# A graph layer's edge rounds on VectorE in another row order, with slot indices decoded in two rounds and 112 first gathers

## The chip, the cores and the metric

The kernel runs on one core of a Trainium2 chip. Five engines matter: TensorE (PE in the profile; PEld is its weight load), VectorE (DVE), ScalarE (ACT), GpSimd (POOL) and SyncE (SP, which only issues transfers). Each works through its own list of instructions in order and waits on semaphores for the others. The metric is device time of one execution in microseconds (us); smaller is better.

## What is computed

A pre-normalised graph layer over 100,000 nodes of 160 features (64 scalars and 32 three-vectors) and 25,000 edges, all in fp32:

```python
h = relu(layernorm(x))                                  # per node, 160 features
s, v = h[:, :64], h[:, 64:].reshape(N, 32, 3)
skip_s, skip_v = s @ W_skip0, einsum('nmi,mk->nki', v, W_skip1)
s, v = s @ W_nl0, einsum('nmi,mk->nki', v, W_nl1)
sh1  = sqrt(3) * edge_attr / norm(edge_attr)            # unit vector of an edge
w    = relu(edge_feature @ W_fc1) @ W_fc2               # 224 weights of an edge, split in 5
xs, xv = s[dst], v[dst]
tp   = concat(w0*xs, w3*dot(xv, sh1)/sqrt(3), (w1*xs) x sh1, w2*xv, w4*cross(xv, sh1)/sqrt(2))
agg  = segment_sum(tp, src) / 32                        # sum over the edges of a node
out_s, out_v = agg_s @ W_out_s + skip_s, agg_v @ W_out_v + skip_v
out  = x + concat(silu(out_s[:, :64]), sigmoid(out_s[:, 64:]) * out_v)
```

## The kernel before

The program has three stages on one time axis.

**Ranking, until about 123 us.** The 25,000 edges stand as 200 tiles of 125 (`NT = 200`). PE and DVE count, tile by tile, how many earlier edges fall into the same bin of nodes; from this rank each edge gets a row of its own in the DRAM tensor `slots`. Meanwhile POOL gathers the node rows of the first edges from `x` by indirect DMA, one call per tile (`gather`, L502), into rings called `xg` and `xb`.

**Edge rounds, about 124 to 590 us.** Four tiles make a group (`GE = 4`, `NG = 50` groups), and all engines run a loop of 53 rounds q, each engine on another group. On DVE `stats_e` takes the layer-norm statistics of a gathered group. For two groups at a time `spread_e`, `squares_e`, `variance_e` (in even rounds) and `guess_e`, `newton_a` to `newton_c`, `shift_e` (in odd rounds) make scale and bias; these are operations on 8 elements per partition, and the last of them, `shift_e`, writes `e_bias` (L685). ACT normalises with it (`norm_e`, L1178, waiting for the semaphore `e_ln`), PE turns and multiplies, and leaves the transformed rows in a PSUM bank (L1329, L1333; semaphore `e_xs`). `products` on DVE then forms the 352 numbers of an edge from the rows in PSUM (`row_s`, `row_v`), the edge's weights `w_sb` and its unit vector `hat` in SBUF: four operations (L853 to L860) read one operand from PSUM and one from SBUF, the eight after them (L864 to L880) read both operands from SBUF. PE projects the result, ACT puts it into a message buffer, and `lift` and `complete` on DVE add one more part to a message of an earlier group (L888, L895, both operands in SBUF) and copy its indices in (L896), which raises `e_fix`.

Then POOL may scatter: `scatter(p)` (L512) waits for `e_fix` of group p and makes four indirect DMA calls, one per tile, from the message buffer into `slots`. POOL's list of calls is written out by hand. First come `FIRST_GATHERS` gather calls. Then POOL waits for the slot indices `sidx` (semaphore `b_slot`, raised by the last of four `slot_rows` steps on DVE, one step at the end of each of the rounds 0 to 3), and goes on with four scatters for each p, followed by the gathers up to `due`:

```python
for p in range(NG):
    scatter(p)
    due = min(NT, max(FIRST_GATHERS + 2 * (p + 1), GE * (p + 10)))
    for m in range(made, due):
        gather(m)
```

With 104 first gathers this is two gathers after each p up to 33 and four after each p from 34 to 40, when all 200 are made; after that only scatters follow. So POOL makes 96 gathers and 200 scatters after the wait for `sidx`.

**Node tiles, from about 590 us.** SP waits until all scatters have landed, loads the slots of each macro tile of 1024 nodes (`mg`), and PE, ACT and DVE compute skip, sum, gate and residual for 98 such tiles. Their instructions are not touched by the change.

Of the kernel before, what the change touches and what calls it, by code (L numbers as in the profile page):

```python
# [5 lines left out]
ALU = mybir.AluOpType  # L6
# [12 lines left out]
def gnn_layer(nc, x, src, dst, edge_vec, edge_feat_t, w_skip0, w_skip1, w_nl0, w_nl1,  # L19
# [10 lines left out]
    GE = 4  # L30
# [36 lines left out]
    FIRST_GATHERS = 104  # L67
# [3 lines left out]
    with ExitStack() as ctx:  # L71
# [289 lines left out]
        with ExitStack() as psum_ctx:  # L361
# [124 lines left out]
            def _(pool):  # L486
# [44 lines left out]
                for p in range(NG):  # L531
                    scatter(p)
                    due = min(NT, max(FIRST_GATHERS + 2 * (p + 1), GE * (p + 10)))
                    for m in range(made, due):
                        gather(m)
                    made = max(made, due)
# [49 lines left out]
            def _(dve):  # L586
# [109 lines left out]
                for t in range(NT):  # L696
# [58 lines left out]
                    if t == 90:  # L755
                        stats_e(2)
                    if t == 100:
# [85 lines left out]
                def products(p, c):  # L843
                    rows = f_x if p == 0 else p_x
                    row_s, row_v = rows[:, :, 0:S], rows[:, :, S:F].rearrange("p t (i k) -> p t i k", i=3)
                    w = w_sb[:, c, :, :]
                    h = hat[:, p * GE:p * GE + GE, :]
                    h3 = h[:, :, 0:3].unsqueeze(3)
                    dve.wait_ge(e_wsb, p + 1)
                    dve.wait_ge(e_xs, p + 1)  # L850
                    wait(dve, e_tp, p)
                    wait(dve, e_tt, GE * (p - 1))
                    dve.tensor_tensor(w4xv[:], w[:, :, W - V:W].unsqueeze(2).to_broadcast((ET, GE, 3, V)),  # L853
                                      row_v, ALU.mult).then_inc(e_w4xv, 1)
                    dve.tensor_tensor(xvh[:], h3.to_broadcast((ET, GE, 3, V)), row_v, ALU.mult).then_inc(e_dot, 1)
                    parts = tp[:, c, :, V + 2 * S:TU].rearrange("p t (i k) -> p t i k", i=3)
                    dve.tensor_tensor(tp[:, c, :, V:V + 2 * S].rearrange("p t (j k) -> p t j k", j=2),
                                      w[:, :, 0:2 * S].rearrange("p t (j k) -> p t j k", j=2),
                                      row_s.unsqueeze(2).to_broadcast((ET, GE, 2, S)), ALU.mult)
                    dve.tensor_tensor(parts[:, :, :, 0:V],  # L860
                                      w[:, :, 2 * S:2 * S + V].unsqueeze(2).to_broadcast((ET, GE, 3, V)),
# [701 lines left out]
```

## Time and profile before

| | |
|---|---|
| median of 3 runs | 1210.98 us (1209.78 to 1215.87) |
| profiled execution | 1209.0 us |
| its span in the profile | 1207.2 us |
| busy share of the span | PE 92%, PEld 78%, DVE 81%, ACT 71%, POOL 60% |
| last scatter call of POOL ends | 586.9 us |
| first load of `mg` issued | 590.5 us |

Times in the rows are counted from the start of the span. A row of the timeline gives the start of an instruction, its duration, the engine, the line, what it does (out <- in, partitions x elements), and in brackets how long the engine stood idle before it and what ended that. POOL shows 0.30 us "issue" ahead of nearly each indirect DMA call: it waits there for nothing that the profile shows. A DVE operation's duration overlaps the start of the next by about 0.08 us in a run of operations that wait for nothing.

### The profile page before, as it was taken

Reading aid. Unit: us, or ns where it says so; the run is one execution under the profiler, and the core shown is the slowest. Engines: PE = TensorE matmul, PEld = TensorE weight load, DVE = VectorE, ACT = ScalarE, POOL = GpSimd, SP = SyncE. Lnnn points to the kernel's source line nnn. Section 1 sums busy time; section 2 is a strip of 40 time slices with the busy share of each in tenths; the row PEclk is TensorE's granted clock in tenths of the full one; section 3 lists DMA queues with packets and bytes.
Section 4 is the critical chain, followed back from the end, with each engine's and each line's share of the span. In section 5 each row is a group of like instructions: output and inputs, shape, how many; then the busy total and the mean of one; then the engine's idle time right before and its main releaser. Section 6 shows DMA issues by size and latency. Waiting matters only on the chain.

```text
span 1207.2 us, 29282 instructions
## 1 busy us (share of the span) xinstructions
PE 1115.1 (92%) x8847; PEld 939.8 (78%) x8847; DVE 979.8 (81%) x3571; ACT 860.4 (71%) x2069; POOL 729.7 (60%) x860
## 2 busy tenths in 40 slices
PE   6989899999999767889699999999999999999996
PEld 4667788888888656778588788888888788888885
DVE  9999898888886447667488888888888888888874
ACT  0300578877777445566598899899888898889984
POOL 6777587787887777777615544554445544554460
PEclk9999899999999788789599999999999999999999
DMA  9999344444446633444387777777777677777763
GB/s 343 404 403 403 119 131 132 129 131 130 130 129 195 214 104 101 114 113 123 106 296 275 259 286 281 282 255 284 284 282 285 247 286 279 285 265 282 286 214 118
DMA packets 108459, 271.12 MB, mean 225 GB/s; under 512 B 13573, under 2 KB 51751, under 8 KB 108364
## 3 DMA queue, kind: packets, MB, share of 16 engines
q1 hardware_dynamic: 87852, 233.20, 54.9%
q0 software_dynamic: 19200, 36.48, 10.4%
q8 instruction: 45, 0.74, 0.2%
q10 hardware_dynamic: 1312, 0.29, 0.1%
q14 instruction: 50, 0.41, 0.1%
HBM read 126.91 MB, written 143.01 MB: 224 GB/s over the span
## 4 chain that ended last, share of the span: by engine, by line
PE 62%; DVE 12%; POOL 12%; issue 8%; DMA 3%; ACT 2%; SPq 0%; DVEq 0%; POOLq 0%; ACTq 0%
PE bank L1465 16%; PE bank L1478 9%; PE bank L1457 8%; POOL slots L512 7%; PE bank L1469 5%; POOL xg L502 5%; PE bank L1394 4%; PE bank L1297 3%; PE bank L1423 3%; PE bank L1329 3%; DVE ob L1047 2%; PE bank L1411 2%; DVE bin_hot L626 2%; PE bank L1407 2%; PE bank L1409 2%
## 5 line engine op out<-in xcount | busy, mean ns | idle before, releaser
L1246 ACT ACTIVATE nn<-xb,n_bias,n_rstd 128x160 f32<-128x160 f32 x784 | 346.2, 528 | 45.3 <-POOL n_bias L567 40.9
L512 POOL DMA_INDIRECT slots<-msg,sidx x200 | 229.3, 1147 | 75.5 <-issue 56.1
L956 DVE BATCH_NORM_STATS2 n_stat<-xb 128x6 f32<-128x160 f32 x784 | 196.0, 312 | 24.8 <-DMA xb<-x 24.2
L1047 DVE SCALAR_TENSOR_TENSOR ob<-sg,bank 128x128 f32<-128x128 f32 x588 | 131.7, 279 | 72.4 <-ACT ob L1261 70.7
L1478 PE MATMUL bank<-mg,hot 64*128 64x192 f32 x1568 | 171.8, 338 | 7.7 <-DVE hot L1032 7.7
L544 POOL TENSOR_TENSOR n_sum<-n_stat 128x32 f32<-128x32 f32 x24 | 6.9, 287 | 279.5 <-DVE n_stat L956 279.5
L502 POOL DMA_INDIRECT xg<-x,dst_i x136 | 145.7, 1072 | 44.0 <-issue 41.0
L561 POOL TENSOR_TENSOR n_rstd<-n_sum,neg_half 128x8 f32<-128x8 f32 x94 | 160.2, 1704 | 5.7 <-issue 2.9
L1465 PE MATMUL bank<-fwd,nt 128*128 128x160 f32 x784 | 144.6, 307 | 14.3 <-DVE ob L1047 12.4
L1253 ACT ACTIVATE nt<-bank 128x640 f32<-128x640 f32 x196 | 137.5, 702 | 18.1 <-PE bank L1458 14.1
L1054 DVE TENSOR_TENSOR ob<-ob,xb 128x1280 f32<-128x1280 f32 x98 | 146.9, 1499 | 3.4
L1457 PE MATMUL bank<-ident,nn 128*128 128x128 f32 x784 | 146.9, 310 | 2.6 <-ACT nn L1246 2.6
L1457 PEld LDWEIGHTS bank<-ident,nn 128*128 128x128 f32 x784 | 109.1, 207 | 46.9 <-issue 46.1
L1465 PE MATMUL bank<-rev,nt 128*128 128x160 f32 x784 | 139.1, 300 | 0.0
L1394 PE MATMUL bank<-ident,tp 125*128 125x125 f32 x600 | 108.3, 291 | 29.4 <-ACT tpt L1202 18.5
L1465 PEld LDWEIGHTS bank<-fwd,nt 128*128 128x128 f32 x784 | 113.0, 191 | 26.1 <-issue 13.4
L1478 PEld LDWEIGHTS bank<-mg,hot 64*128 64x128 f32 x1568 | 124.4, 188 | 7.9 <-DVE hot L1032 7.9
L1394 PEld LDWEIGHTS bank<-ident,tp 125*128 125x128 f32 x600 | 70.9, 150 | 64.3 <-issue 25.8
L1202 ACT ACTIVATE tpt<-bank 128x375 f32<-128x375 f32 x200 | 96.3, 482 | 31.9 <-PE bank L1394 31.5
L1465 PEld LDWEIGHTS bank<-rev,nt 128*128 128x128 f32 x784 | 117.7, 191 | 0.0
L638 DVE BATCH_NORM_STATS2 e_stat<-xg 125x6 f32<-125x160 f32 x136 | 37.1, 313 | 66.8 <-DMA xg<-x,dst_i 66.8
L1178 ACT ACTIVATE hn<-xg,e_bias,e_rstd 125x160 f32<-125x160 f32 x136 | 63.4, 523 | 37.0 <-DVE e_bias L685 37.0
(191 smaller groups left out, 2669.9 us busy)
## 6 DMA issues: line engine op xcount, KB each, us to landing
xb<-x SPq DMA_DIRECT2D x97, 640.0 KB, 5.1
out_dram<-ob SPq DMA_DIRECT2D x97, 640.0 KB, 3.3
slots<-blank SPq DMA_DIRECT2D x14, 2744.0 KB
mg<-slots SPq DMA_DIRECT2D x98, 392.0 KB, 4.0
messages<-msg SPq DMA_DIRECT2D x50, 382.8 KB
ef<-edge_feat_t SPq DMA_DIRECT2D x50, 125.0 KB
slots<-msg,sidx POOLq DMA_INDIRECT x200, 4.1
xg<-x,dst_i POOLq DMA_INDIRECT x136, 6.8
```

Of the source, the lines that this page charges most:

```text
L502: pool.indirect_dma_start(rows_of(g)[:, t, :], None, x[:, :], bass.IndirectOffsetOnAxis(ap=dst_i[:, m:m + 1], axis=0)).then_inc(e_x[g % XS ...
L512: pool.indirect_dma_start(slots[:, :], bass.IndirectOffsetOnAxis(ap=sidx[:, m:m + 1], axis=0), msg[:, c, t, 0:MW], None).then_inc(e_sc[c], 16)
L561: pool.tensor_tensor(n_rstd[:, b, cols], n_sum[:, b, 4, cols], neg_half[:], ALU.pow).then_inc(n.chain, 1)
L956: done = dve.bn_stats(n_stat[:, u // U, u % U * G + g, :], xb[:, u, g, :])
L1047: last = dve.scalar_tensor_tensor(out=o[:, :, S + V * j:S + V * j + V], in0=sg[:, h, :, :], scalar=1.0, in1=z[:, :, part], op0=ALU.add, op ...
L1054: dve.tensor_tensor(o, o, xb[:, u, :, :], ALU.add).then_inc(n.res, 1)
L1246: last = act.activation(nn[:, u % 2, h, spread_of(g % 4)], xb[:, u, g, order_of(g % 4)], ACT.Relu, bias=n_bias[:, u // U, c:c + 1], scale= ...
L1253: act.activation(nt[:, h, :], q_t[h], ACT.Relu).then_inc(n.ht, 1)
L1394: last = pe.transpose(p_tt[:, i * ET:(i + 1) * ET], tp[:, c, t, TURN[i]:TURN[i] + P], idt)
L1457: pe.transpose(q_t[h][:, t * P:(t + 1) * P], nn[:, u % 2, h, main_of(t)], ident[:])
L1465: pe.matmul(z[:, t, 0:F], nt[:, h, t * P:(t + 1) * P], sides[t // 2][:, skip_cols], start=(t % 2 == 0), stop=False, skip_group_check=True)
L1478: last = pe.matmul(q_z[h][:, t, 0:Z], hot[slots, u % 2, pair, :], mg[slots, u % U, pair, 0:Z], start=False, stop=True, skip_group_check=True)
```

## The change

Nothing is computed differently; instructions stand in another order. Four things move.

1. `FIRST_GATHERS` is 112 in place of 104, and `due` has `p + 11` in place of `p + 10`.
2. Two of the four `slot_rows` steps stand at the end of round 0 and two at the end of round 1, so `sidx` is written at the end of round 1 and not of round 3.
3. `stats_e(3)` moves from round 0 into the ranking stage (at t = 96; `stats_e(2)` from t = 90 to t = 88), and each round takes the statistics of group q + 4 as its last work where the next round took them as its first.
4. `products`, `lift` and `complete` are dissolved into one round body. Their operations and the small ones alternate, so that the four that read PSUM stand between those whose operands are both in SBUF.

The core of the diff, cut:

```diff
-    FIRST_GATHERS = 104
+    FIRST_GATHERS = 112
...
-                    due = min(NT, max(FIRST_GATHERS + 2 * (p + 1), GE * (p + 10)))
+                    due = min(NT, max(FIRST_GATHERS + 2 * (p + 1), GE * (p + 11)))
...
-                    if t == 90:
+                    if t == 88:
                         stats_e(2)
+                    if t == 96:
+                        stats_e(3)
...
                 def round_e(q):
-                    m = q // 2 + 1
...
-                    if within(q - 1):
-                        products(q - 1, (q + 1) % 2)
-                    if q < 4:
-                        slot_rows(q)
+                    p, c, m = q - 1, (q + 1) % 2, q // 2 + 1
+                    root, spread = q % 2 == 1 and within(q + 1), q % 2 == 0 and within(q + 3)
+                    r = q - 3
+
+                    if root:
+                        guess_e(m)
+                    if spread:
+                        spread_e(m)
+                    if within(r):
+                        h3 = hat[:, r * GE:r * GE + GE, 0:3].unsqueeze(3).to_broadcast((ET, GE, 3, V))
+                        v = msg[0:ET, r % MR, :, SG:Z].rearrange("p t (i k) -> p t i k", i=3)
+                        dve.wait_ge(e_msb, 2 * r + 2)
+                        wait(dve, e_fix, r)
+                        dve.tensor_tensor(hu[:], msg[0:ET, r % MR, :, Z:Z + V].unsqueeze(2).to_broadcast((ET, GE, 3, V)), h3,
+                                          ALU.mult).then_inc(e_hu, 1)
+                    if root:
+                        newton_a(m)
+                    if spread:
+                        squares_e(m)
+                    if within(p):
+                        rows = f_x if p == 0 else p_x
+                        row_s, row_v = rows[:, :, 0:S], rows[:, :, S:F].rearrange("p t (i k) -> p t i k", i=3)
+                        w = w_sb[:, c, :, :]
+                        h = hat[:, p * GE:p * GE + GE, :]
+                        parts = tp[:, c, :, V + 2 * S:TU].rearrange("p t (i k) -> p t i k", i=3)
+                        dve.wait_ge(e_wsb, p + 1)
+                        dve.wait_ge(e_xs, p + 1)
+                        wait(dve, e_tp, p)
+                        wait(dve, e_tt, GE * (p - 1))
+                        dve.tensor_tensor(xvh[:], h[:, :, 0:3].unsqueeze(3).to_broadcast((ET, GE, 3, V)), row_v, ALU.mult
+                                          ).then_inc(e_dot, 1)
+                    if root:
+                        newton_b(m)
+                    if spread:
+                        variance_e(m)
+                    if within(r):
+                        dve.wait_ge(e_hu, r + 1)
+                        dve.tensor_tensor(v, v, hu[:], ALU.add)
+                        dve.tensor_copy(msg[0:ET, r % MR, :, LOCAL:NODE + 1], place_of[:, r * GE:r * GE + GE, :]).then_inc(e_fix, 1)
+                    if root:
+                        newton_c(m)
+                    if within(p):
+                        dve.tensor_tensor(w4xv[:], w[:, :, W - V:W].unsqueeze(2).to_broadcast((ET, GE, 3, V)),
+                                          row_v, ALU.mult).then_inc(e_w4xv, 1)
+                        dve.wait_ge(e_dot, 3 * p + 1)
+                        dve.tensor_tensor(dot[:, 0, :, :], xvh[:, :, 0, :], xvh[:, :, 1, :], ALU.add).then_inc(e_dot, 1)
+                        dve.tensor_tensor(tp[:, c, :, V:V + 2 * S].rearrange("p t (j k) -> p t j k", j=2),
+                                          w[:, :, 0:2 * S].rearrange("p t (j k) -> p t j k", j=2),
+                                          row_s.unsqueeze(2).to_broadcast((ET, GE, 2, S)), ALU.mult)
+                        dve.wait_ge(e_w4xv, p + 1)
+                        dve.tensor_tensor(cr_a[:, :, 0:2, :], w4xv[:, :, 1:3, :],
+                                          h[:, :, 2:4].unsqueeze(3).to_broadcast((ET, GE, 2, V)), ALU.mult)
+                        dve.tensor_tensor(cr_a[:, :, 2, :], w4xv[:, :, 0, :],
+                                          h[:, :, 1:2].to_broadcast((ET, GE, V)), ALU.mult)
+                    if root:
+                        shift_e(m)
+                    if within(p):
+                        dve.tensor_tensor(parts[:, :, :, 0:V],
+                                          w[:, :, 2 * S:2 * S + V].unsqueeze(2).to_broadcast((ET, GE, 3, V)),
+                                          row_v[:, :, ::-1, :], ALU.mult).then_inc(e_px, 1)
+                        dve.wait_ge(e_dot, 3 * p + 2)
+                        dve.tensor_tensor(dot[:, 1, :, :], dot[:, 0, :, :], xvh[:, :, 2, :], ALU.add).then_inc(e_dot, 1)
+                        dve.tensor_tensor(cr_b[:, :, 0, :], w4xv[:, :, 2, :], h[:, :, 1:2].to_broadcast((ET, GE, V)), ALU.mult)
+                        dve.tensor_tensor(cr_b[:, :, 1:3, :], w4xv[:, :, 0:2, :],
+                                          h[:, :, 2:4].unsqueeze(3).to_broadcast((ET, GE, 2, V)), ALU.mult).then_inc(e_cross, 1)
+                        dve.wait_ge(e_dot, 3 * p + 3)
+                        dve.tensor_tensor(tp[:, c, :, 0:V], dot[:, 1, :, :],
+                                          w[:, :, 2 * S + V:2 * S + 2 * V], ALU.mult)
+                        dve.wait_ge(e_cross, p + 1)
+                        dve.tensor_tensor(parts[:, :, :, V:2 * V],
+                                          cr_a[:, :, ::-1, :], cr_b[:, :, ::-1, :], ALU.subtract).then_inc(e_tp, 1)
+                    if within(q + 4):
+                        stats_e(q + 4)
+                    if q < 2:
+                        slot_rows(2 * q)
+                        slot_rows(2 * q + 1)
```

On DVE, an odd round stood before in this order from `newton_c` (L681) on (`BN_STATS` is the last of its statistics, L685 is `shift_e`, L888 is `lift`, L895 and L896 are `complete`, L853 begins `products`):

```order
L681 SCALAR_TENSOR_TENSOR e_rstd<-e_step,e_rstd 125x8
L638 BN_STATS e_stat<-xg 125x6
L685 SCALAR_TENSOR_TENSOR e_bias<-e_sum,e_rstd 125x8
L888 TENSOR_TENSOR hu<-msg,hat 125x384
L895 TENSOR_TENSOR msg<-msg,hu 125x4x96
L896 COPY msg<-place_of 125x4x2
L853 TENSOR_TENSOR w4xv<-w_sb,bank 125x384
```

and in the changed kernel, from the operation that follows `newton_a` on (L876 was L855, L884 was L895, L885 was L896, L889 was L853, L892 was L864, L893 was L857, L897 and L899 were L867 and L869, L904 was L860):

```order
L876 TENSOR_TENSOR xvh<-hat,bank 125x384
L675 SCALAR_TENSOR_TENSOR e_step<-e_root,e_sum 125x8
L884 TENSOR_TENSOR msg<-msg,hu 125x4x96
L885 COPY msg<-place_of 125x4x2
L681 SCALAR_TENSOR_TENSOR e_rstd<-e_step,e_rstd 125x8
L889 TENSOR_TENSOR w4xv<-w_sb,bank 125x384
L892 TENSOR_TENSOR dot<-xvh 125x128
L893 TENSOR_TENSOR tp<-w_sb,bank 125x4x128
L897 TENSOR_TENSOR cr_a<-w4xv,hat 125x4x64
L899 TENSOR_TENSOR cr_a<-w4xv,hat 125x4x32
L685 SCALAR_TENSOR_TENSOR e_bias<-e_sum,e_rstd 125x8
L904 TENSOR_TENSOR tp<-w_sb,bank 125x4x3x32
```

The bias of the next two groups (L685) stood ahead of all products of its round; now it stands behind `lift`, `complete` and six of the twelve operations of `products`.

The last part of `products` on DVE stood before as eight operations with both operands in SBUF behind the last one that reads PSUM (`bank`):

```order
L860 TENSOR_TENSOR tp<-w_sb,bank 125x4x3x32
L864 TENSOR_TENSOR dot<-xvh 125x128
L867 TENSOR_TENSOR cr_a<-w4xv,hat 125x4x64
L869 TENSOR_TENSOR cr_a<-w4xv,hat 125x4x32
L872 TENSOR_TENSOR dot<-dot,xvh 125x128
L873 TENSOR_TENSOR cr_b<-w4xv,hat 125x4x32
L874 TENSOR_TENSOR cr_b<-w4xv,hat 125x4x64
L877 TENSOR_TENSOR tp<-dot,w_sb 125x4x32
L880 TENSOR_TENSOR tp<-cr_a,cr_b 125x4x3x32
```

and in the changed kernel as

```order
L904 TENSOR_TENSOR tp<-w_sb,bank 125x4x3x32
L908 TENSOR_TENSOR dot<-dot,xvh 125x128
L909 TENSOR_TENSOR cr_b<-w4xv,hat 125x4x32
L910 TENSOR_TENSOR cr_b<-w4xv,hat 125x4x64
L913 TENSOR_TENSOR tp<-dot,w_sb 125x4x32
L916 TENSOR_TENSOR tp<-cr_a,cr_b 125x4x3x32
L638 BN_STATS e_stat<-xg 125x6 x4
```

Three of the eight (L864, L867, L869) moved ahead of the last PSUM operation; five still stand in one run, and the statistics follow them.

On POOL the calls from the end of the ranking stage on stood before as

```order
L524 IOTA sidx 128x200
L502 DMA xg<-x,dst_i 128x160 x66
L502 DMA xb<-x,dst_i 128x160 x36
L512 DMA slots<-msg,sidx 50776x196 x4
L502 DMA xb<-x,dst_i 128x160 x2
```

and now as

```order
L524 IOTA sidx 128x200
L502 DMA xg<-x,dst_i 128x160 x66
L502 DMA xb<-x,dst_i 128x160 x44
L512 DMA slots<-msg,sidx 50776x196 x4
L502 DMA xb<-x,dst_i 128x160 x2
```

(two gathers more stand ahead of the IOTA in both). Eight gathers moved ahead of the first scatter; the end of POOL's list of calls, as a difference, shows where they are gone:

```order
-L512 DMA slots<-msg,sidx 50776x196 x4
-L502 DMA xg<-x,dst_i 128x160 x4
-L512 DMA slots<-msg,sidx 50776x196 x36
+L512 DMA slots<-msg,sidx 50776x196 x40
 L544 TENSOR_TENSOR n_sum<-n_stat 128x32
```

The last gather now follows scatter p = 39 and not p = 40, so 88 gathers and 160 scatters stand between the wait for `sidx` and the last gather, where 96 and 164 stood; 40 scatters follow it, not 36.

## Rows read from the trace of the kernel before

**Rows 1.** Who waited for whom, POOL, 5 to 600 us: total, times, longest.
```profile
POOL slots L512 <- DVE sidx L809: 10.0, 1, 10.0
POOL slots L512 <- DVE msg L896: 9.4, 15, 5.2
```

**Rows 2.** Who waited for whom, all engines, 386 to 532 us: the longest.
```profile
DVE e_stat L638 <- DMA xg<-x,dst_i: 63.2, 11, 9.5
```

**Rows 3.** Timeline of POOL: four of the calls that mark its stages.
```profile
147.82 1.01 POOL L512 DMA_INDIRECT slots<-msg,sidx  x1 [9.97 <-DVE sidx L809]
...
386.05 0.96 POOL L502 DMA_INDIRECT xg<-x,dst_i  x1 [0.31 <-issue]
...
530.75 0.95 POOL L502 DMA_INDIRECT xg<-x,dst_i  x1 [0.30 <-issue]
...
585.97 0.97 POOL L512 DMA_INDIRECT slots<-msg,sidx  x1 [0.30 <-issue]
```

**Rows 4.** Timeline of POOL in two steady rounds: three prolonged calls, one undisturbed.
```profile
202.84 1.32 POOL L512 DMA_INDIRECT slots<-msg,sidx  x1 [0.30 <-issue]
204.47 0.99 POOL L512 DMA_INDIRECT slots<-msg,sidx  x1 [0.30 <-DVE msg L896]
...
207.03 1.90 POOL L512 DMA_INDIRECT slots<-msg,sidx  x1 [0.30 <-issue]
...
222.39 1.93 POOL L512 DMA_INDIRECT slots<-msg,sidx  x1 [0.30 <-issue]
```

**Rows 5.** Timeline of DVE in the same stretch: one odd round.
```profile
202.72 0.56 DVE L888 TENSOR_TENSOR hu<-msg,hat 125x384 f32<-125x384 f32 x1 [0.82 <-ACT msg L1211]
203.32 0.56 DVE L895 TENSOR_TENSOR msg<-msg,hu 125x384 f32<-125x384 f32 x1
203.79 0.34 DVE L896 COPY msg<-place_of 125x8 f32<-125x8 f32 x1
203.87 0.55 DVE L853 TENSOR_TENSOR w4xv<-w_sb,bank 125x384 f32<-125x384 f32 x1
204.33 0.55 DVE L855 TENSOR_TENSOR xvh<-hat,bank 125x384 f32<-125x384 f32 x1
204.79 0.68 DVE L857 TENSOR_TENSOR tp<-w_sb,bank 125x512 f32<-125x512 f32 x1
205.39 0.54 DVE L860 TENSOR_TENSOR tp<-w_sb,bank 125x384 f32<-125x384 f32 x1
205.86 0.28 DVE L864 TENSOR_TENSOR dot<-xvh 125x128 f32<-125x128 f32 x1
206.06 0.41 DVE L867 TENSOR_TENSOR cr_a<-w4xv,hat 125x256 f32<-125x256 f32 x1
206.40 0.28 DVE L869 TENSOR_TENSOR cr_a<-w4xv,hat 125x128 f32<-125x128 f32 x1
206.60 0.28 DVE L872 TENSOR_TENSOR dot<-dot,xvh 125x128 f32<-125x128 f32 x1
...
207.54 0.55 DVE L880 TENSOR_TENSOR tp<-cr_a,cr_b 125x384 f32<-125x384 f32 x1
```

**Rows 6.** Timeline of ACT in the same odd round.
```profile
204.85 0.94 ACT L1178 ACTIVATE hn<-xg,e_bias,e_rstd 125x160 f32<-125x160 f32 x2
206.13 0.48 ACT L1202 ACTIVATE tpt<-bank 128x375 f32<-128x375 f32 x1 [0.33 <-PE bank L1394]
206.73 0.54 ACT L1211 ACTIVATE msg<-bank 125x448 f32<-125x448 f32 x1
207.17 0.93 ACT L1178 ACTIVATE hn<-xg,e_bias,e_rstd 125x160 f32<-125x160 f32 x2
```

**Rows 7.** Timeline of PE: the rows' last product, and the next turn of normalised rows.
```profile
203.23 0.27 PE L1333 MATMUL bank<-rev,ht 64*125 64x64 f32 x1
...
208.18 0.73 PE L1379 MATMUL bank<-ident,hn 125*128 125x125 f32 x4
```

**Rows 8.** Timeline of DVE: the operation that completes the last message.
```profile
578.97 0.30 DVE L896 COPY msg<-place_of 125x8 f32<-125x8 f32 x1
```

More of the change, by code:

```diff
@@ L883, in lift @@
-                def lift(p):
-                    c = p % MR
-                    h3 = hat[:, p * GE:p * GE + GE, 0:3].unsqueeze(3).to_broadcast((ET, GE, 3, V))
-                    dve.wait_ge(e_msb, 2 * p + 2)
-                    wait(dve, e_fix, p)
-                    dve.tensor_tensor(hu[:], msg[0:ET, c, :, Z:Z + V].unsqueeze(2).to_broadcast((ET, GE, 3, V)), h3,
-                                      ALU.mult).then_inc(e_hu, 1)
-                def complete(p):
-                    c = p % MR
-                    v = msg[0:ET, c, :, SG:Z].rearrange("p t (i k) -> p t i k", i=3)
-                    dve.wait_ge(e_hu, p + 1)
-                    dve.tensor_tensor(v, v, hu[:], ALU.add)
-                    dve.tensor_copy(msg[0:ET, c, :, LOCAL:NODE + 1], place_of[:, p * GE:p * GE + GE, :]).then_inc(e_fix, 1)
@@ L898, in round_e @@
-                def round_e(q):
-                    m = q // 2 + 1
-                    if q % 2 == 0:
-                        if within(q + 3):
-                            stats_e(q + 3)
-                            spread_e(m)
-                        if within(q - 3):
-                            lift(q - 3)
-                        if within(q + 3):
-                            squares_e(m)
-                        if within(q - 3):
-                            complete(q - 3)
-                        if within(q + 3):
-                            variance_e(m)
-                    else:
-                        more = within(q + 1)
-                        if more:
-                            guess_e(m)
-                        if within(q + 3):
-                            stats_e(q + 3, range(0, 1))
-                        if more:
-                            newton_a(m)
-                        if within(q + 3):
-                            stats_e(q + 3, range(1, 2))
-                        if more:
-                            newton_b(m)
-                        if within(q + 3):
-                            stats_e(q + 3, range(2, 3))
-                        if more:
-                            newton_c(m)
-                        if within(q + 3):
-                            stats_e(q + 3, range(3, 4))
-                        if more:
-                            shift_e(m)
-                        if within(q - 3):
-                            lift(q - 3)
-                            complete(q - 3)
-                    if within(q - 1):
-                        products(q - 1, (q + 1) % 2)
-                    if q < 4:
-                        slot_rows(q)
```

38 lines of the change are left out of this document (removed).

## The prediction

> **What bounds the kernel now.** I read the waits first, engine by engine, then the chain that ended last, then the timelines of POOL and of the three engines it meets. The node stage after 590 us is untouched by the change and needs the last scatter, so its length stays and the question is when the last scatter ends: at 585.97 + 0.97 = 586.94 us [rows 3]. POOL has nothing to wait for between its first gather and that moment except 10.0 us for `sidx` and 9.4 us for completed messages, of which 5.2 us lie in one wait near the end [rows 1]. From 386 us on it is DVE that waits for gathered rows, 63.2 us in 11 times [rows 2]. So the edge stage is POOL's list of calls; PE, ACT and DVE run ahead of it until the gathers are short, and follow it from then on.
>
> The list has three stretches [rows 3]. The first scatter starts at 147.82, and the call at 386.05 is the 156th after the wait (26 times four scatters and two gathers): 155 calls in 238.2 us, 1.537 us each, while DVE is full. The call after the one at 530.75 starts 0.95 + 0.30 later, at 532.00: 105 calls in 145.95 us, 1.390 each, while DVE is half idle. The last 36 scatters take 54.94 us, 5.2 of it the one wait: 1.383 each. A call that meets nothing costs its 0.95 to 1.01 us and 0.30 us of issue, about 1.28 us.
>
> Why 1.537 and not 1.28: in a steady pair of rounds two kinds of call are prolonged [rows 4]. The one at 202.84 starts 0.12 us into L888 (202.72), and ends at 204.16, 0.88 after L888 [rows 5]. The one at 207.03 starts in the middle of the run from L869 to L880 and ends at 208.93, 0.84 after L880 ended at 208.09. With some 0.98 us for a call by itself they were let in at 203.18 and 207.95, 0.10 and 0.14 us before those operations ended. So a call that starts inside a DVE operation with both operands in SBUF first waits, and in the run from L869 to L880 (208.09 - 206.40 = 1.69 us) it waits for the whole of what is left of the run. The call at 204.47 starts beside L855, which reads PSUM, and takes 0.99. From 207.03 to 222.39, two rounds later, POOL makes 10 calls: 15.36 / 10 = 1.536, the rate of the whole stretch.
>
> At this place the Trainium skill has a rule, in "SBUF — State Buffer", section "SBUF: two separate sides": a VectorE operation with two SBUF inputs and a GpSimd operation that reads SBUF share a port pair as an exclusive lock, held for one whole instruction. The trace agrees that such operations block a call [rows 4, 5]; it disagrees on one instruction, since the call at 207.03 waited through several. By the rule no call would be held longer than one operation, at most 0.55 us, in either order, and the new order would end where the first rival below does; by the rows it can gain in rate only if no run is longer than the 1.28 us between two calls.
>
> **The change part by part.**
>
> *112 first gathers.* POOL was free from 147.82 - 9.97 = 137.85 on. Eight more gathers fill that wait: 8 x 1.25 (0.95 + 0.30) = 10.0 us, so 147.9; DVE is in its first rounds then, and one hit on the run costs up to 1.6 us. I take 149.5 for the first scatter, 1.7 us later than before (bounds 0 and 3). `sidx` is ready earlier and hides behind these gathers: the first message was complete before the last of four steps released POOL at 147.82, and the two steps in round 1 come some 15 us, two rounds, earlier. If it were late after all, it costs at most the two rounds it gained.
>
> *Fewer calls ahead of the last gather.* 88 gathers and 160 scatters, 248 calls, in place of 260; then 40 scatters in place of 36.
>
> *The new DVE order and POOL's rate.* The operations are the same, so the time that locks are held is about the same, but it stands in pieces: `lift` alone, L895 alone (0.47 us each), L864 alone (0.2), L867 and L869 (0.54), and the run from L872 to L880, 208.09 - 206.60 = 1.49 us, of which about 1.37 bar a new call (the last 0.1 did not, above). This run is still longer than 1.28, so each round catches a call in it. After release the next starts follow at 1.28, 2.56, 3.84, 5.12 and 6.40 us; the next run starts one round less 1.37 us later. For a round of 7.68 that is 6.31: the fifth start falls just inside, so five calls per round, as now. What the short pieces add falls into slack ahead of that hit.
>
> *The late bias.* In odd rounds `e_bias` now stands behind xvh, L895, L896, w4xv, L864, L857, L867 and L869. From start to start these take 0.46 + 0.47 + 0.08 + 0.46 + 0.20 + 0.60 + 0.34 + 0.20 = 2.81 us [rows 5], two small operations 0.08 each (as L896 to L853), and I put 0.2 for `shift_e` itself until ACT sees it. xvh can start when the rows are done, 203.23 + 0.27 = 203.50 [rows 7], say 203.65. So the bias is ready at 206.8, where ACT started to normalise at 204.85: 1.95 late. Between ACT's first and second pair of normalisations there are 2.32 us, 0.33 of it idle and about 0.2 more a wait inside 206.13 to 206.73 [rows 6], so the second slips by some 1.4 us. PE's turn at 208.18 came right behind it (207.17 + 0.93 = 208.10), and PE is full: a pair of rounds grows from 15.36 to 16.76 us. Bounds: nothing, if PE's order takes it up, and 1.95. In front of ACT's normalisation then stand its copies for PE (L1202), so PE's projection waits too; that is the same 1.4, not a second one. For POOL a round of 9.08 and one of 7.68 take 6 and 5 calls by the reckoning above (9.08 - 1.37 = 7.71, sixth start at 7.68, at the edge of the run): 11 calls in 16.76, 1.524 each. The change to the order thus leaves POOL's rate as it was.
>
> *Statistics.* Group q + 4 at the end of round q is the same place as the start of round q + 1; `stats_e(3)` moves 1 us from round 0 into the ranking stage. Nothing, as DVE is in the path in both.
>
> **The sum.** First, when do gathers run short? DVE needs group 4 at about 124 us, when the ranking ends, and one group a round from then on. Before: group 26 + j was complete after 12(j + 1) calls, 147.8 + 18.4(j + 1) + 1 for landing, and needed at 124 + 7.68(22 + j): equal at j = 11.7, 383 us; the trace has 386. After: 149.5 + 18.3(j + 1) + 1 against 126 + 8.38(24 + j), with 2 us for the late bias in the first rounds: j = 16.0, 461 us. Until then (461 - 149.5) / 1.524 = 204 calls. The remaining 44 ahead of the last gather go at 1.390, 61 us: 522. The 40 scatters take 40 x 1.383 = 55 us: 577. Does the last message hold them up? It was complete at 579.27 [rows 8], 48.5 us after the start of the last gather; now 520.3 + 48.5 + 1.4 = 570.2, and with four more calls 575.3: just hidden. So 577 against 586.94: 10 us less. The node stage follows as before. Own time 1209.0 - 10 = 1199; the median of the runs is 2.0 us above the profiled execution, so on it 1201.
>
> In other terms: 8 calls fewer at 1.39 (11 us) and the wait of 5.2 gone, less 1.7 at the start and 49 more calls at the full-DVE rate (49 x 0.14 = 7): about 8 to 10.
>
> **The rivals.**
>
> *The gaps do open.* A sixth call fits into each round, because one start slips in ahead of the run (it misses by 0.03 to 0.09 us in the reckoning) or because locks go operation by operation. For it: the edge is that thin. Against: the run is still over 1.28, and 155 calls before kept their ten per pair. With 12 calls per pair, 1.397: short at 487 us, last gather done at 496, POOL could end at 551. Then the rounds themselves bind: group 49 read at 126 + 45 x 8.38 = 503, its message some 47 + 1.4 later, four calls: 557. That is 30 us less, 1181. The rule of the Trainium skill named above, one instruction per lock, would end here as well.
>
> *One more hit per pair (the other side).* The five pieces of lock now lie about 1.3 us apart, near POOL's own step, so a released call can run into the next piece, again and again. Ten calls in 16.76 us, 1.676: short at 439 us, 173 calls; 75 x 1.39 = 105, last gather at 544, end 599: 12 us more, 1223. It decides from 1.59 per call on, 10.5 calls a pair; there the gain is gone. For it: the pieces add up to as much as before, in rounds whose length changes. Against: a hit on a short piece costs 0.2 to 0.4 and mostly eats the slack ahead of the long one.
>
> *The late bias binds.* If PE loses over 2.7 us per pair (a round of 9.05) the rounds end after POOL does: 126 + 45 x 9.05 + 48.4 + 5.1 = 587, no gain, and slower beyond. For it: three engines hang on the moved operation. Against: the rows bound the loss by 1.95. About 1205 to 1218.
>
> **How the numbers follow.** Forecast 50 in 100, by itself 1193 to 1207; gaps open 22; one more hit 14; late bias 14. Changes of under 0.5% (6 us, so 1205 to 1217) cannot be told from none here. Faster by more: 0.45 of the forecast, all of the open gaps, a little of the late bias: 0.68. Within: 0.05, 0.02 and 0.10 of the others: 0.17. Slower: 0.15. The range 1182 to 1214 leaves out about half of the open gaps and most of the one more hit.
>
> **What would show it.** First scatter at 148 to 151 us with no wait on `sidx`. POOL's calls between 160 and 440 us at 1.50 to 1.55 us from start to start, with one call of about 2 us a round that ends 0.85 us after the subtraction L916. ACT's normalisation waiting for L685 some 2 us in each odd round; in PE a gap of about 1.4. DVE's wait for gathers beginning near 460 and far below 63 us. The last gather at 520, the last scatter at 577. I am wrong if POOL's rate in the full stretch leaves 1.45 to 1.6, if rounds are longer than 9 us, or if the node stage changes length.

## The result and the profile after

| kernel | median | ratio to before, 95% interval | profiled execution, its span |
|---|---|---|---|
| before | 1212.65 us (4 runs, 1209.78 to 1215.87) | | 1209.0, 1207.2 us |
| after | 1181.89 us (4 runs, 1181.02 to 1182.06) | 0.9744 (0.9716 to 0.9773) | 1181.0, 1179.2 us |

The change takes 31 us off, three times the forecast of 10, and ends 0.1 us below the range. It came out at the time of the first rival, *the gaps do open*.

In the timeline of POOL after, these are the marks of the stages, as in [rows 3] before (start, duration, engine, line, operation, idle time ahead of it and what ended it):

```profile
148.49 1.24 POOL L512 DMA_INDIRECT slots<-msg,sidx  x1 [0.30 <-issue]
...
495.32 0.95 POOL L502 DMA_INDIRECT xg<-x,dst_i  x1 [0.30 <-issue]
...
548.67 0.97 POOL L512 DMA_INDIRECT slots<-msg,sidx  x1 [5.50 <-DVE msg L885]
...
557.65 0.97 POOL L512 DMA_INDIRECT slots<-msg,sidx  x1 [0.30 <-issue]
```

The first scatter starts right behind the first gathers, the last gather comes 35.4 us earlier than before (530.75), and the last scatter ends at 558.62, 28.3 us earlier (586.94). The rest of the span is as long as it was: 1179.2 - 558.6 = 620.6 against 620.3 us. So the whole gain lies in the edge stage. From 148.49 to 495.32 there are 247 calls, 1.404 us each; the forecast had 1.524 while VectorE is full.

Three answers on who waited for whom after: POOL from 5 to 600 us (against [rows 1]), then DVE from 386 to 532 us (against [rows 2]), then ACT from 160 to 380 us; total, times, longest:

```profile
POOL slots L512 <- DVE msg L885: 14.1, 21, 5.5
```

```profile
DVE hu L860 <- ACT msg L1195: 21.0, 14, 2.9
```

```profile
ACT hn L1162 <- DVE e_bias L685: 23.7, 13, 1.8
```

POOL no longer waits for `sidx`. DVE's 63.2 us of waiting for gathered rows are gone; what it waits for longest there are ACT's messages. And between 160 and 380 us a wait is there that the kernel before did not have in that stretch: ACT stands 1.8 us in each odd round for the late `e_bias`.

This is POOL after in one steady pair of rounds (against [rows 4]), all twelve calls up to the one with which the pattern begins again:

```profile
208.69 1.11 POOL L502 DMA_INDIRECT xb<-x,dst_i  x1 [0.30 <-issue]
210.11 0.96 POOL L502 DMA_INDIRECT xb<-x,dst_i  x1 [0.30 <-issue]
211.38 1.00 POOL L512 DMA_INDIRECT slots<-msg,sidx  x1 [0.30 <-issue]
212.69 0.99 POOL L512 DMA_INDIRECT slots<-msg,sidx  x1 [0.30 <-issue]
213.98 0.97 POOL L512 DMA_INDIRECT slots<-msg,sidx  x1 [0.30 <-DVE msg L885]
215.25 1.13 POOL L512 DMA_INDIRECT slots<-msg,sidx  x1 [0.30 <-issue]
216.69 1.65 POOL L502 DMA_INDIRECT xb<-x,dst_i  x1 [0.30 <-issue]
218.63 0.97 POOL L502 DMA_INDIRECT xb<-x,dst_i  x1 [0.30 <-issue]
219.91 1.00 POOL L512 DMA_INDIRECT slots<-msg,sidx  x1 [0.30 <-issue]
221.22 0.99 POOL L512 DMA_INDIRECT slots<-msg,sidx  x1 [0.31 <-issue]
222.51 0.97 POOL L512 DMA_INDIRECT slots<-msg,sidx  x1 [0.30 <-issue]
223.79 1.20 POOL L512 DMA_INDIRECT slots<-msg,sidx  x1 [0.30 <-issue]
225.29 1.12 POOL L502 DMA_INDIRECT xb<-x,dst_i  x1 [0.30 <-issue]
```

Twelve calls in 225.29 - 208.69 = 16.60 us, 1.383 each, where ten stood in 15.36. Two calls fall on VectorE's last run, as forecast. But only one of them is long (1.65); the one at 208.69 takes 1.11. The run that it met, on DVE (against [rows 5]):

```profile
208.13 0.29 DVE L908 TENSOR_TENSOR dot<-dot,xvh 125x128 f32<-125x128 f32 x1
208.33 0.29 DVE L909 TENSOR_TENSOR cr_b<-w4xv,hat 125x128 f32<-125x128 f32 x1
208.53 0.42 DVE L910 TENSOR_TENSOR cr_b<-w4xv,hat 125x256 f32<-125x256 f32 x1
208.87 0.29 DVE L913 TENSOR_TENSOR tp<-dot,w_sb 125x128 f32<-125x128 f32 x1
209.07 0.56 DVE L916 TENSOR_TENSOR tp<-cr_a,cr_b 125x384 f32<-125x384 f32 x1
209.53 0.33 DVE L638 BATCH_NORM_STATS2 e_stat<-xg 125x6 f32<-125x160 f32 x1
```

The call ends at 209.80. With 0.97 for a call by itself it was let in at 208.83, 0.12 us before the end of L910 and in the middle of the run. The call at 216.69 met the same operations 7.86 us later:

```profile
215.99 0.28 DVE L908 TENSOR_TENSOR dot<-dot,xvh 125x128 f32<-125x128 f32 x1
...
216.39 0.41 DVE L910 TENSOR_TENSOR cr_b<-w4xv,hat 125x256 f32<-125x256 f32 x1
...
216.93 0.55 DVE L916 TENSOR_TENSOR tp<-cr_a,cr_b 125x384 f32<-125x384 f32 x1
...
224.72 0.29 DVE L908 TENSOR_TENSOR dot<-dot,xvh 125x128 f32<-125x128 f32 x1
```

It was held to 217.37, 0.11 us before the end of L916. (The prediction found calls let in 0.10 and 0.14 us before the end of an operation; "at the end" means this below.) I had taken it that every call is held to the end of the run. The two rounds from run to run last 7.86 and 8.73 us; the forecast had 7.68 and 9.08.

**Counting it over the steady stretch.** From each POOL call between 160 and 380 us I took 0.97 off and put what was left, if over 0.06, to the DVE operation inside which the call starts (the later one where two overlap). Before: 143 calls, 37.0 us lost; 30 calls on the last run (L864 to L880) lose 29.7 us, of which 28 that start in its `cr_b` products 29.3 us (1.05 each); 27 on `hu` lose 7.2 us. After: 156 calls, 20.5 us lost; 26 calls on the last run lose 14.7 us (0.57 each), 22 on `cr_a` 4.4 us. Each round still catches a call on its run, but at half the price: in 10 of the 26 the call was let in at the end of the operation in which it started (durations of 1.10 to 1.12), in the others at the end of the run. Before, all of the 28 were held to the end of the run, one of them beyond it. On the short piece L897, L899, too, both ways occur: of the 12 calls that start in L897, 11 were let in at its end, though L899 follows at once, and one at the end of L899.

### The profile page after: what moved, and what is told of

It reads as the page before. It is cut to its first block, busy times and chain, and to the rows that moved or that the text cites. A ratio compares the mean times of both kernels' runs of the same rounds, so it can differ in the third digit from the quotient of the medians.

```text
span 1179.2 us, 29282 instructions
## 1 busy us (share of the span) xinstructions
PE 1099.4 (93%) x8847; PEld 922.8 (78%) x8847; DVE 980.9 (83%) x3571; ACT 855.6 (73%) x2069; POOL 707.7 (60%) x860
## 4 chain that ended last, share of the span: by engine, by line
PE 65%; DVE 20%; issue 7%; ACT 4%; DMA 2%; POOL 1%; SPq 0%; DVEq 0%; ACTq 0%; POOLq 0%
PE bank L1449 16%; PE bank L1462 9%; PE bank L1441 8%; PE bank L1378 5%; PE bank L1453 5%; PE bank L1313 4%; PE bank L1281 3%; PE bank L1391 3%; DVE ob L1031 3%; PE bank L1395 3%; PE bank L1363 2%; DVE n_stat L940 2%; PE bank L1393 2%; PE bank L1407 2%; DVE bin_hot L626 2%
## 5 line engine op out<-in xcount | busy, mean ns | idle before, releaser
L512 POOL DMA_INDIRECT slots<-msg,sidx x200 | 215.1, 1075 | 68.6 <-issue 54.5
L502 POOL DMA_INDIRECT xg<-x,dst_i x136 | 138.3, 1017 | 44.4 <-issue 44.1
L1449 PEld LDWEIGHTS bank<-fwd,nt 128*128 128x128 f32 x784 | 113.1, 192 | 25.6 <-issue 12.1
L1378 PE MATMUL bank<-ident,tp 125*128 125x125 f32 x600 | 104.4, 284 | 21.6 <-ACT tpt L1186 21.1
L1453 PE MATMUL bank<-fwd,nt 64*128 64x64 f32 x392 | 85.0, 297 | 0.0
```

Of the source, the lines that this page charges most:

```text
L502: pool.indirect_dma_start(rows_of(g)[:, t, :], None, x[:, :], bass.IndirectOffsetOnAxis(ap=dst_i[:, m:m + 1], axis=0)).then_inc(e_x[g % XS ...
L512: pool.indirect_dma_start(slots[:, :], bass.IndirectOffsetOnAxis(ap=sidx[:, m:m + 1], axis=0), msg[:, c, t, 0:MW], None).then_inc(e_sc[c], 16)
L1378: last = pe.transpose(p_tt[:, i * ET:(i + 1) * ET], tp[:, c, t, TURN[i]:TURN[i] + P], idt)
L1449: pe.matmul(z[:, t, 0:F], nt[:, h, t * P:(t + 1) * P], sides[t // 2][:, skip_cols], start=(t % 2 == 0), stop=False, skip_group_check=True)
L1453: pe.matmul(z[:, 2 * j:2 * j + 2, F:Z], nt[part, h, 4 * P:5 * P], sides[j][part, skip_z_cols], start=False, stop=every, skip_group_check=True)
```

## The experiments

Theories: **G**, the gaps between VectorE's operations on two SBUF operands set POOL's rate, and this is most of the gain; **L**, the list of calls brought it; and, for what is left in after, **R**, the late bias bounds the rounds, against **P**, POOL's calls do. Each ratio is to runs of before on the same chip; these had medians of 1212.65 us (for after), 1217.41 us (for the first four experiments) and 1216.97 us (for the last three). "Pair" is the mean time of two rounds between 160 and 380 us, "lost" is counted as above.

| kernel | ratio, 95% interval | pair | calls in 160 to 380 | lost us (on the last run) | last gather | last scatter ends |
|---|---|---|---|---|---|---|
| before | 1 | 15.37 | 143 | 37.0 (29.7) | 530.8 | 586.9 |
| after | 0.9744 (0.9716 to 0.9773) | 16.72 | 156 | 20.5 (14.7) | 495.3 | 558.6 |
| e1_list | 0.9882 (0.9845 to 0.9919) | 15.37 | 143 | 36.8 (29.8) | 519.8 | 576.1 |
| e2_order | 0.9879 (0.9841 to 0.9917) | 16.73 | 156 | 18.9 (13.2) | 512.8 | 575.1 |
| e3_bias | 0.9699 (0.9667 to 0.9730) | 15.37 | 156 | 20.1 (18.0) | 494.1 | 550.7 |
| e4_join | 0.9897 (0.9864 to 0.9930) | 17.18 | 146 | 32.2 (27.1) | 518.0 | 584.9 |
| e5_join2 | 0.9755 (0.9722 to 0.9789) | 15.37 | 151 | 24.0 (21.7) | 504.8 | 562.8 |
| e6_spread | 0.9479 (0.9447 to 0.9512) | 15.37 | 169 | 3.2 (no such run left) | 474.6 | 537.0 |
| e7_stat | 0.9609 (0.9572 to 0.9646) | 15.37 | 164 | 10.2 (4.3) | 484.8 | 552.2 |

**The list alone.** The edit to the kernel before:

```diff
-    FIRST_GATHERS = 104
+    FIRST_GATHERS = 112
...
-  due = min(NT, max(FIRST_GATHERS + 2 * (p + 1), GE * (p + 10)))
+  due = min(NT, max(FIRST_GATHERS + 2 * (p + 1), GE * (p + 11)))
...
-  if q < 4:
-      slot_rows(q)
+  if q < 2:
+      slot_rows(2 * q)
+      slot_rows(2 * q + 1)
```

> The kernel before with the list of calls alone changed: 112 first gathers, gathers due by p + 11, slot rows in two rounds; VectorE's order is the old one. Theory G (the new order's gaps raised POOL's rate, the list is a small part): POOL stays at 10 calls per steady pair of 15.36 us, 1.536 each; 248 instead of 260 calls stand ahead of the last gather, which takes some 8 to 10 us off: 1202 to 1206. Rival L (the list did it; the order matters little): 1182 to 1190.

Measured 1201.56 us, ratio 0.9882. POOL's rate is that of before to the call (143), and the last scatter ends 10.9 us earlier. This is the part of the change that I had forecast, and at the last scatter its size was right; on the median time it is 15.9 us, with an interval of 10 to 19.

**The order alone.** After, with those three edits taken back.

> The kernel after with the old list: 104 first gathers, gathers due by p + 10, slot rows in four rounds; VectorE's order is the new one. Theory G: 12 calls per pair of 16.6 us, 1.383 each, as after. About 257 calls from 148 us on stand ahead of the last gather, which then starts at 148 + 257 x 1.383 = 503; group 49 is needed at about 500, so the rows are just short, by some 5 us, and the time is 1184 to 1192. Rival L: POOL is back near 1.5 per call, 1200 to 1213.

Measured 1201.29 us, ratio 0.9879. The order makes 156 calls out of 143 without the list, so L is wrong: the order is worth 1.2%. But the list is worth as much, so G is right on POOL's rate and not in its second half: the gaps are half of the gain, not most of it. It gained less than expected: POOL waited 14.3 us for `sidx` and began at 151.69, the last gather came at 512.8 and not 503, and DVE waited 20.8 us for rows and not 5. The two parts add up, 1.2% and 1.2% against 2.6% together, within their intervals.

**The bias early.**

```diff
 if root:
     guess_e(m)
+    newton_a(m)
+    newton_b(m)
+    newton_c(m)
+    shift_e(m)
 ...
-if root:
-    newton_a(m)
 ...
-if root:
-    shift_e(m)
```

(`newton_b` and `newton_c` leave their old places too.)

> The kernel after with the chain of the root (guess to shift) run in one piece ahead of the odd round's first large product, so that the bias is ready some 5 us earlier; all else as after. Theory R (after the change the rounds are the bound, through the late bias; POOL only follows): the pair falls from 16.60 to 15.4 us and POOL comes along with 12 calls per pair at the floor of 1.28; 22 pairs x 1.2 = up to 27 us less, 1155 to 1165, or less where the gathers run short. Rival P (POOL, at 1.383, binds the pair itself): pair and time as after, 1180 to 1184. Rival S (in a pair of 15.4 us some calls hit VectorE's run again): 11 or 10 calls per pair, 1.40 to 1.54 each, 1172 to 1200.

Measured 1179.49 us, ratio 0.9699. These are the rows of the windows view from 160 to 380 us, after first and then e3_bias; the columns are the stretch, its length, the busy time of PE, PEld, DVE, ACT and POOL with their instructions, PE's granted clock (share of full speed), the DMA engines' share and GB/s:

```profile
160.00:380.00 220.00, 208.84 (x1661) 179.41 (x1661) 180.31 (x657) 158.41 (x355) 172.46 (x157) 0.99 0.48 130
```

```profile
160.00:380.00 220.00, 220.00 (x1803) 191.87 (x1803) 201.02 (x713) 174.46 (x388) 172.46 (x157) 1.00 0.51 136
```

With the early bias PE is busy all the time, the pair is back at 15.37, and ACT's wait for `e_bias` is gone. So the late bias did bind the rounds of after (R), and what bounds a pair from below is PE. But POOL makes the same number of calls in the same time, 156, and the gain over after is small, and in the ratios not clear of the noise (0.9699 against 0.9744, the intervals overlap, on two chips): DVE is now waiting for gathers 22.9 us in 386 to 532. P is right as well: in after the two bounds lie close together. And the pair's length is not what lets more calls in: e1_list and e3_bias have the same list and the same pair of 15.37, and 143 against 156 calls. What differs is VectorE's order.

Two rows of POOL in e3_bias show how thin the line is:

```profile
255.68 0.96 POOL L502 DMA_INDIRECT xg<-x,dst_i  x1 [0.30 <-issue]
...
263.43 2.14 POOL L502 DMA_INDIRECT xg<-x,dst_i  x1 [0.30 <-issue]
```

and DVE's operations in which they start, with the next one, and the end of the second run:

```profile
255.50 0.28 DVE L904 TENSOR_TENSOR dot<-dot,xvh 125x128 f32<-125x128 f32 x1
255.70 0.31 DVE L905 TENSOR_TENSOR cr_b<-w4xv,hat 125x128 f32<-125x128 f32 x1
...
263.25 0.28 DVE L904 TENSOR_TENSOR dot<-dot,xvh 125x128 f32<-125x128 f32 x1
263.45 0.28 DVE L905 TENSOR_TENSOR cr_b<-w4xv,hat 125x128 f32<-125x128 f32 x1
...
264.66 0.54 DVE L638 BATCH_NORM_STATS2 e_stat<-xb 125x6 f32<-125x160 f32 x2
```

Both start 0.18 us into L904. The first goes through, and L905 is 0.03 longer; the second is held for the whole run, to 264.60.

**One product moved back, late bias.** After, with:

```diff
+ dve.tensor_tensor(parts[:, :, :, 0:V], w ..., row_v ..., ALU.mult).then_inc(e_px, 1)
  dve.wait_ge(e_w4xv, p + 1)
  dve.tensor_tensor(cr_a[:, :, 0:2, :], ...)
  dve.tensor_tensor(cr_a[:, :, 2, :], ...)
  ...
- dve.tensor_tensor(parts[:, :, :, 0:V], w ..., row_v ..., ALU.mult).then_inc(e_px, 1)
  dve.tensor_tensor(dot[:, 1, :, :], ...)
```

> The kernel after with one product that reads PSUM (tp from the bank's rows, 384 elements) moved from between the cross products back ahead of them: the run of operations on SBUF operands at the end of a round becomes 7 operations, some 2.0 us, in place of 5, some 1.35; same work, same number of operations. If a whole run is held against POOL: one call per round is held 0.6 us longer, 11 or 10 calls per pair, 1.5 to 1.66 each, and 1190 to 1215. If the lock goes operation by operation: 12 calls per pair and 1180 to 1184.

Measured 1205.03 us, ratio 0.9897: one operation at another place gives back most of the gain, and the calls fall to 146. But the move also put one more product ahead of `shift_e`. ACT's wait for it grew from 1.8 to 29.6 / 13 = 2.3 us and the pair to 17.18. And in the odd rounds `shift_e` still stands between the `cr_a` products and the rest, so the run of seven stands in the even rounds alone. Two things were changed at once, so it was done again on e3_bias.

**The same move, early bias.** The same edit, on e3_bias.

> The kernel of e3_bias (early bias, pair 15.37 us, POOL at 1.37 to 1.43 per call) with the one product on PSUM rows moved back ahead of the cross products, so that the last run of SBUF operations is 7 long, 2.0 us, and not 5, 1.4; in e4_join the same move also made the bias later still, here it does not. If runs are held as a whole: pair stays 15.37 and POOL falls back to some 1.5 per call (10 to 10.5 a pair), as in the kernel before; 1195 to 1208. If what made e4_join slow was its longer pair alone: POOL at 1.40 and 1177 to 1184.

Measured 1188.86 us, ratio 0.9755, between the two expectations. The pair did not move (15.37); calls fell from 156 to 151, the last scatter ends 12.1 us later, and the time rose by some 0.6% (0.9755 against 0.9699; the intervals overlap a little, and the chips were two). A longer run costs calls, then, but much less than I had expected of whole runs being held: of 29 calls that start in it, 9 still pass after one operation (8 of them of the 20 that start in the sum L904). By difference, the rest of e4_join's loss came with the later bias; no run shows that by itself.

**The run cut up.** On e3_bias, the same operations in this order (a star marks those that read PSUM):

```diff
- *w4xv, dot0, *tp, cr_a, cr_a, *parts, dot1, cr_b, cr_b, tp(V), sub
+ dot0, *w4xv, cr_a, cr_a, dot1, *tp, cr_b, cr_b, tp(V), *parts, sub
```

> The kernel of e3_bias with the last run cut up: sums, cross products and the last product stand in five pieces, none over 0.75 us (0.47, 0.75, 0.74, 0.74, 0.46), each behind an operation that reads PSUM; same operations. If a call's price is what is left of the run in which it starts, no call is held over 0.75 us: 1.30 to 1.37 per call, 11.2 to 11.8 a pair of 15.37, POOL's 288 calls after 148 us end 10 to 25 us earlier: 1155 to 1170. If only the sum of the held time counts (it is the same as in e3_bias): 1.40 and 1176 to 1183. If the later release of PSUM costs PE its rows: the pair grows over 15.5 and the time is over 1180.

Measured 1155.40 us, ratio 0.9479, in the range of the first expectation: the fastest kernel here. A piece of the timeline of DVE in it, and POOL's calls beside it:

```profile
259.44 0.42 DVE L892 TENSOR_TENSOR cr_a<-w4xv,hat 125x256 f32<-125x256 f32 x1
259.78 0.28 DVE L894 TENSOR_TENSOR cr_a<-w4xv,hat 125x128 f32<-125x128 f32 x1
259.99 0.28 DVE L898 TENSOR_TENSOR dot<-dot,xvh 125x128 f32<-125x128 f32 x1
260.19 0.68 DVE L899 TENSOR_TENSOR tp<-w_sb,bank 125x512 f32<-125x512 f32 x1
260.79 0.28 DVE L902 TENSOR_TENSOR cr_b<-w4xv,hat 125x128 f32<-125x128 f32 x1
260.99 0.42 DVE L903 TENSOR_TENSOR cr_b<-w4xv,hat 125x256 f32<-125x256 f32 x1
261.32 0.29 DVE L906 TENSOR_TENSOR tp<-dot,w_sb 125x128 f32<-125x128 f32 x1
261.52 0.55 DVE L908 TENSOR_TENSOR tp<-w_sb,bank 125x384 f32<-125x384 f32 x1
261.99 0.55 DVE L912 TENSOR_TENSOR tp<-cr_a,cr_b 125x384 f32<-125x384 f32 x1
```

```profile
259.09 0.97 POOL L512 DMA_INDIRECT slots<-msg,sidx  x1 [0.30 <-DVE msg L885]
260.36 0.98 POOL L502 DMA_INDIRECT xg<-x,dst_i  x1 [0.30 <-issue]
261.65 0.96 POOL L502 DMA_INDIRECT xg<-x,dst_i  x1 [0.30 <-issue]
262.92 1.00 POOL L512 DMA_INDIRECT slots<-msg,sidx  x1 [0.30 <-issue]
```

169 calls from 160 to 380 us, 1.304 each, with 3.2 us lost in all. With the same operations and the same time spent on SBUF operands, what counts is how long they stand together. Fewer calls were prolonged (18, in e3_bias 37), and each by less (0.18 us on the mean against 0.54); this run does not separate the two. No wait of DVE for gathered rows is left in the edge stage. POOL waits for DVE's messages 24.1 us in 35 times between 5 and 600 us: now the rounds are the bound, and PE is busy in all of these 220 us.

**An operation with one SBUF operand in the run.** On e3_bias:

```diff
  dve.tensor_tensor(cr_b[:, :, 1:3, :], ...).then_inc(e_cross, 1)
+ if within(q + 4):
+     stats_e(q + 4, range(0, 1))
  dve.wait_ge(e_dot, 3 * p + 3)
  ...
- stats_e(q + 4)
+ stats_e(q + 4, range(1 if within(p) else 0, GE))
```

> The kernel of e3_bias with one of the four statistics operations (one operand, 0.25 us) moved from behind the last run into its middle, so that the run is 0.74 + 0.66 us with an operation between that has one SBUF operand and not two. If such an operation lets a waiting call in as one on PSUM does: hits of at most 0.75 us, 1.31 to 1.38 per call, 1160 to 1175. If it does not, the run is held through it and is 0.25 longer: 1.42 to 1.50 per call, 1182 to 1195.

Measured 1171.77 us, ratio 0.9609: 164 calls, 1.345 each. Here the run of e3_bias is cut by one statistics operation of 0.24 us (261.72 to 261.96). Of the calls that start in the run or in that operation none takes over 1.60 us, where 13 took over 2 us in e3_bias; of six that start in its first operation two were not held, and four, of 1.47 to 1.53 us, were let in where the statistics operation begins. So was this one:

```profile
261.55 1.11 POOL L512 DMA_INDIRECT slots<-msg,sidx  x1 [0.31 <-issue]
```

```profile
261.39 0.43 DVE L906 TENSOR_TENSOR cr_b<-w4xv,hat 125x256 f32<-125x256 f32 x1
261.72 0.33 DVE L638 BATCH_NORM_STATS2 e_stat<-xb 125x6 f32<-125x160 f32 x1
261.96 0.28 DVE L911 TENSOR_TENSOR tp<-dot,w_sb 125x128 f32<-125x128 f32 x1
```

It was let in at 262.66 - 0.97 = 261.69. So the statistics operation, which reads one SBUF operand, lets POOL in, as one that reads PSUM does.

That does not hold for every operation with one SBUF operand. In after, a call starts inside one of the `TENSOR_SCALAR` operations that stand in one round only; they read one SBUF operand of whole numbers:

```profile
167.24 1.35 POOL L512 DMA_INDIRECT slots<-msg,sidx  x1 [0.30 <-issue]
```

```profile
167.09 0.43 DVE L822 TENSOR_SCALAR digits<-whole_i 125x196 int32<-125x196 int32 x2
167.43 0.26 DVE L824 TENSOR_SCALAR digits<-whole_i 125x196 int32<-125x196 int32 x1
```

It was let in at 168.59 - 0.97 = 167.62, through three such operations and 0.07 us before the last one ends.

## Why the prediction was wrong

*What bounds the kernel: right.* POOL's list of calls set the edge stage, and calls are prolonged by DVE's operations on two SBUF operands: with the list and the pair the same, the order alone made 156 calls out of 143 (e3_bias against e1_list), and cutting up the run takes the loss from 20.1 to 3.2 us in 220.

*112 first gathers, and fewer calls ahead of the last gather: right.* First scatter 148.49 (149.5 forecast) with no wait for `sidx`. The list alone brought 10.9 us at the last scatter; the forecast of the whole change was 10.

*The new order and POOL's rate: this is the step that failed.* It said that each round catches a call on the run from L872 to L880, and that the call is held to the run's end, so that a pair of 16.76 us has 11 calls, 1.524 each, and that the order thus leaves POOL's rate as it was. A steady pair has 12 calls, 1.383 each, below the 1.45 that the prediction had named as a sign of being wrong. The first half holds: 26 calls in some 26 rounds. The second does not: they lost 0.57 us each and not about 1.05 as before; 10 of them were let in at the end of the operation in which they started. I had read "held to the end of the run" from a kernel in which all of 28 calls were, and made a rule of it.

The reckoning could not tell 11 calls from 12 in any case. By its own figures the sixth start of the longer round, at 7.68, comes 0.03 us ahead of the run at 7.71 and is not held, which makes 7 + 5 = 12; I had counted it as held. The split of the pair was off as well: with rounds of 7.86 and 8.73 us the run begins at 6.49 and 7.36 after the release, the fifth start at 6.40 is ahead of it in both, and the count is 6 + 6 = 12 even if every call is held to the end, by a margin of 0.09 us. So the runs do not show which of the two, the early release or the split, gave after its twelfth call. What the early release spares by itself can be estimated: in after 10 calls some 0.67 us each, 6.7 of the 16.5 us by which after lost less than before; in e3_bias 8 calls 1.2 us and 4 calls 0.7, some 12 of the 16.7 us by which it lost less than e1_list, at the same list and pair. I gave the one side 50 and the other 22 where the margin allowed no such odds; and the first rival met the time, but neither of its two reasons is what the runs show in full.

The rule of the Trainium skill that I weighed there ("SBUF — State Buffer", section "SBUF: two separate sides": the lock is held for one instruction) would by the prediction's reckoning have given 12 calls, the result. The runs bear out neither it nor my reading in full: 10 of 26 calls on the run are let in after one operation, as it says, and 11 of 12 on L897; the other 16 and 1 are held to the end of their run.

*The late bias: right in the pair's length, not in how it splits.* ACT waits 23.7 / 13 = 1.8 us for it (1.95 forecast), and the pair is 16.60 in the steady rounds, 16.72 on the mean (16.76); but the shorter round grew too (7.86), and PE idles 220 - 208.84 = 11.2 us in the stretch, some 0.85 a pair where a gap of 1.4 was expected. That it bound the rounds of after was not in my forecast but in the rival's; e3_bias shows that it did, and that it cost little, since POOL was not faster.

*When gathers run short: follows from the failed step.* At 1.404 us per call the last gather came at 495.32, about when its rows were needed, so DVE never waited for rows (the forecast had a shortage from 461 us, the last gather at 522). Then the rounds were the end: the last message was complete here,

```profile
550.65 0.31 DVE L885 COPY msg<-place_of 125x8 f32<-125x8 f32 x1
```

28.3 us ahead of [rows 8]. POOL's last wait is that of 5.50 us ahead of the call at 548.67, for the message of the group before; eight calls follow it without another, and the last message was complete 2.9 us before its own four calls began at 553.84. The forecast had that wait gone and the messages hidden behind POOL.

*The node stage: right*, 620.6 against 620.3 us.

The rival *one more hit per pair* needed over 1.59 us per call; no kernel here came near it on the mean over the steady stretch (e4_join, the slowest of the new order, has 1.505).

## What to carry to other kernels

Where GpSimd's descriptor calls bind beside a busy VectorE, look for the calls in the timeline that take longer than the rest and for the operations under them. It is not the total of VectorE's work on two SBUF operands that counts but how long such operations stand in one piece: put those that read PSUM, or statistics operations, between them. With pieces of some 0.75 us, against POOL's step of 1.28, 3.2 of 220 us were lost here. When a count hangs on a margin of a few hundredths of a microsecond, give both counts like chances. And when an order is changed for one engine, look at what small operation (here `e_bias`) was carried behind the large ones, and put it back in front.

## What was not expected of the hardware

- A call that meets a run of DVE operations on two SBUF operands is let in either at the end of the operation in which it starts or at the end of the whole run. In the kernels before, after, e3_bias, e4_join and e5_join2 nearly all calls on the last run are of one of these two kinds. Two calls at the same 0.18 us into the same operation went either way (0.96 and 2.14 us, above). For the longer `cr_b` product the place of the start goes with the outcome: in after and e2_order the 20 calls that start 0.16 to 0.18 us into L910 are let in at its end, and the 22 that start at 0.09 to 0.10 or 0.29 to 0.31 are held to the end of the run. In the kernel before no call started there: 10 started 0.02 to 0.03 us into the same product and 18 in the one ahead of it. That all were held there may be the luck of where they fell; no run tests it. One call against this (e5_join2, 0.18 us into L906, held), and the starts at 0.18 us above, show that the place alone does not decide; what does stays open.
- A statistics operation with one SBUF operand of 160 elements per partition, 0.24 us long, is enough of a gap: with it in the run, calls took 1.345 us from start to start in place of 1.405. `TENSOR_SCALAR` operations with one SBUF operand are no gap: a call that started in one was held through three (167.24, above).
- In e6_spread POOL's calls came to 1.304 us from start to start over 220 us, of which 0.30 is issue, beside a DVE that was busy 204.03 of those 220 us: a full VectorE is no hindrance by itself.
